# Two loads of the joined stage issued by ScalarE instead of SyncE

## The reference, cut to what matters

```python
def step(carry, inp):                      # one chunk: 16 tokens, 4 batches, 8 heads
    W1c, b1c = carry
    xq, xk, xv, et = inp
    Z1 = xk @ W1c + b1c
    grad = _ln_l2_bwd(Z1, xv - xk, g, bb)
    Attn1 = jnp.tril(xq @ xk.swapaxes(-1, -2))
    b1_bar = b1c - jnp.tril(et) @ grad
    Z1_bar = xq @ W1c - et * Attn1 @ grad + b1_bar
    last_eta = et[..., -1, :, None]
    W1n = W1c - (last_eta * xk).swapaxes(-1, -2) @ grad
    b1n = b1c - (last_eta * grad).sum(-2, keepdims=True)
    return ((W1n, b1n), xq + _ln(Z1_bar, g, bb, EPS_IN))
```

## Time and profile before

| | |
|---|---|
| median of 3 runs | 6032.22 us (6026.91 to 6053.81) |
| profiled execution | 6036.71 us |
| its span, first to last instruction | 6034.6 us |
| mean granted TensorE clock | 0.937 |
| busy: PE, PEld | 5435.4, 3858.9 us (90%, 64%) |
| busy: DVE | 3921.2 us (65%) |
| busy: ACT, POOL | 2358.1, 2375.7 us (39% each) |
| DMA queue 1 (SP's) | 613160 packets, 541.06 MB |
| DMA queue 10 (ACT's) | 157904 packets, 144.22 MB |

### The profile page before, as it was taken

How to read it: one execution, slowest core, us unless ns; L and a number is a source line. 1 busy time by engine, 2 the same in 40 slices (tenths; PEclk the granted TensorE clock), 3 DMA queues, 4 the chain that set the end, 5 groups by cost and what they waited for, 6 DMA issues and landing times. The chain is left out here.

```text
span 6034.6 us, 139327 instructions
## 1 busy us (share of the span) xinstructions
PE 5435.4 (90%) x42562; PEld 3858.9 (64%) x42562; DVE 3921.2 (65%) x14040; ACT 2358.1 (39%) x6645; POOL 2375.7 (39%) x3910
## 2 busy tenths in 40 slices
PE   5999999999688888898888888897899999599999
PEld 2444444444377777777777777777666666377777
DVE  5666666656677777777777777776566666444444
ACT  0111111111255555555555555554333333233333
POOL 1444444444355555555555555553112222122221
PEclk8999999999788988989889999998999999799999
DMA  4444444343345544545455455453212211122221
GB/s 176 159 142 143 138 155 144 120 130 124 105 118 124 126 121 124 125 123 125 122 125 127 120 127 127 126 127 93 113 77 90 89 62 61 66 91 90 90 90 72
DMA packets 771865, 694.46 MB, mean 115 GB/s; under 512 B 334160, under 2 KB 672472, under 8 KB 760184
## 3 DMA queue, kind: packets, MB, share of 16 engines
q1 hardware_dynamic: 613160, 541.06, 31.2%
q10 hardware_dynamic: 157904, 144.22, 7.1%
HBM read 402.96 MB, written 282.20 MB: 114 GB/s over the span
## 5 line engine op out<-in xcount | busy, mean ns | idle before, releaser
L1496 PE MATMUL proj_ps<-proj_w_sb,proj_h 128*128 128x512 f32 x3072 | 1351.1, 598 | 0.0
L1496 PEld LDWEIGHTS proj_ps<-proj_w_sb,proj_h 128*128 128x128 f32 x3072 | 580.4, 192 | 746.6 <-issue 727.4
L2287 PE MATMUL scan_ps_y<-scan_o_t,proj_wo_sb 128*128 128x128 f32 x4096 | 614.0, 296 | 2.1 <-ACT scan_o_t L1920 2.1
L1399 DVE SCALAR_TENSOR_TENSOR proj_lin<-proj_ps,proj_rstd,proj_wbias_sb 128x512 f32<-128x512 f32 x384 | 283.8, 747 | 500.9 <-PE proj_ps L1496 495.1
L1823 POOL TENSOR_TENSOR scan_b_step<-scan_core,scan_rate_last 128x128 f32<-128x128 f32 x512 | 321.9, 629 | 617.1 <-DVE scan_core L2076 616.8
L2287 PEld LDWEIGHTS scan_ps_y<-scan_o_t,proj_wo_sb 128*128 128x128 f32 x4096 | 532.2, 203 | 47.8 <-ACT scan_o_t L1920 2.6
L1884 ACT ACTIVATE scan_square<-scan_ps_z 128x64 f32<-128x64 f32 x1024 | 217.9, 219 | 719.4 <-PE scan_ps_z L2205 700.1
L1877 ACT COPY scan_state_w<-scan_ps_w 128x512 f32<-128x512 f32 x480 | 280.8, 585 | 328.1 <-PE scan_ps_w L2217 323.4
L2217 PE MATMUL scan_ps_w<-scan_step,scan_record 64*128 64x128 f32 x4088 | 383.1, 310 | 24.5 <-DVE scan_step L2081 23.6
L1308 POOL TENSOR_TENSOR proj_by_cos<-proj_lin,proj_rope 128x512 f32<-128x512 f32 x256 | 333.2, 1315 | 167.9 <-DVE proj_lin L1399 126.0
L2055 DVE TENSOR_TENSOR scan_zg<-scan_ps_z,scan_gain 128x128 f32<-128x128 f32 x512 | 145.9, 285 | 386.2 <-ACT scan_square L1884 326.0
(11 more groups left out here) (317 smaller groups left out, 12143.3 us busy)
## 6 DMA issues: line engine op xcount, KB each, us to landing
scan_record<-records SPq DMA_DIRECT2D x258, 392.0 KB
records<-proj_rec ACTq DMA_DIRECT2D x256, 392.0 KB, 3.6
spectra<-fourier_spec SPq DMA_DIRECT2D x16, 2112.0 KB, 6.5
fourier_spec<-spectra SPq DMA_DIRECT2D x16, 2112.0 KB, 8.2
scan_k_in<-records SPq DMA_DIRECT2D x258, 128.0 KB, 5.3
proj_h<-x SPq DMA_DIRECT2D x32, 1024.0 KB, 6.6
queries<-proj_q ACTq DMA_DIRECT2D x128, 256.0 KB, 3.7
gradients<-scan_stored SPq DMA_DIRECT2D x512, 64.0 KB
```

The costliest lines, as they stand in the source:

```text
L1399: v.scalar_tensor_tensor(lin[q][:, n], ps[q][n][:], rstd[k][:, j:j + 1], T.wbias[:, n], ALU.mult, ALU.add).then_inc(lin_sb.sem, 1)
L1496: last = pe.matmul(ps[j % 2][n][:], h[k][:, ct, j * P:(j + 1) * P], T.w[:, n, ct], start=ct == 0, stop=ct == CT - 1)
L2287: pe.matmul(ps_y[:, n], T.wo[:, ct, n * P:(n + 1) * P], o_t[:, ct], start=ct == 0, stop=False)
```

## The change

The second load of the keys, and the load of the queries, leave SP's body and stand in ACT's. The keys: in every even step but the very first (c = 0 included), between `leave` and `outputs_turned`, for the slot that has just ended, with the same wait for `turn_k`. The queries: at c = 4, right behind the keys, instead of at c = 3. SP's last wait for `k_loaded` goes to ACT. The load that the last odd step issued for a tile beyond the end is gone with it (one of 129).

```diff
--- SP's body
-                elif scan:
-                    if c == 3:
-                        if isinstance(v, int) and not p:
-                            sp.wait_ge(turn_k.sem, turn_k.at(B, 0))
-                        if not isinstance(v, int):
-                            sp.wait_ge(qb_sb.sem, qb_sb.at(v * 8 + p * 4 - 4, 0))
-                        sp.dma_start(q_sb[p][:]..., q_in[:, bass.ds((v * 2 + p) * P, P)]...).then_inc(q_loaded[p].sem, 16)
-                    b, n = (c // 2 + 1) % B, p + 1 + (c // 2 + 1) // B
-                    sp.wait_ge(turn_k.sem, turn_k.at(v * 8 + at.slot + 1 + B, 0))
-                    load_keys(k_in[:], k_loaded, b, v * 2 + n)
--- ACT
+            def load_keys(at):
+                b, n = (at.slot + 1) % B, 1 + (at.slot + 1) // B
+                act.wait_ge(turn_k.sem, turn_k.at(at.v * 8 + at.slot + 1 + B, 0))
+                for n2 in range(2):
+                    act.dma_start(k_in[:].rearrange("p (a n) e -> p a n e", n=2)[:, :, n2],
+                                  rec[:, bass.ds((at.v * 2 + n) * P, P), n2, b, n2 * HD:(n2 + 1) * HD].rearrange("a t e -> t a e")
+                                  ).then_inc(k_loaded.sem, 16)
+            def load_queries(at):
+                if isinstance(at.v, int) and not at.p:
+                    act.wait_ge(turn_k.sem, turn_k.at(B, 0))
+                if not isinstance(at.v, int):
+                    act.wait_ge(qb_sb.sem, qb_sb.at(at.v * 8 + at.p * 4 - 4, 0))
+                act.dma_start(q_sb[at.p][:]..., q_in[:, bass.ds((at.v * 2 + at.p) * P, P)]...).then_inc(q_loaded[at.p].sem, 16)
--- ACT's body, even steps
                     if gone:
                         leave(gone)
+                    if scan and not (isinstance(at.s, int) and at.s == 0):
+                        load_keys(Place(at.v, at.p, at.c - 1) if at.c else Place(at.v - 1 + at.p, 1 - at.p, 7))
+                    if scan and at.c == 4:
+                        load_queries(at)
                     if proj:
                         outputs_turned(proj)
```

More of the change, by code:

```diff
@@ L1779, in body @@
                                 "o (a t n) e -> n (o t) a e", n=2, t=CS)[n]).then_inc(grad_in[q].sem, 16)
-                elif scan:
-                    if c == 3:
-                        if isinstance(v, int) and not p:
-                            sp.wait_ge(turn_k.sem, turn_k.at(B, 0))
-                        if not isinstance(v, int):
-                            sp.wait_ge(qb_sb.sem, qb_sb.at(v * 8 + p * 4 - 4, 0))
-                        sp.dma_start(q_sb[p][:].rearrange("p b h e -> p b (h e)"), q_in[:, bass.ds((v * 2 + p) * P, P)].rearrange("b n c -> n b c")
-                                     ).then_inc(q_loaded[p].sem, 16)
-                    b, n = (c // 2 + 1) % B, p + 1 + (c // 2 + 1) // B
-                    sp.wait_ge(turn_k.sem, turn_k.at(v * 8 + at.slot + 1 + B, 0))
-                    load_keys(k_in[:], k_loaded, b, v * 2 + n)
             loop(sp, body)
@@ L1800, in _ @@
                     sp.wait_ge(grad_gone[g][q].sem, grad_gone[g][q].at(SC * 4, 0))
-            sp.wait_ge(k_loaded.sem, k_loaded.at(TILES + 1, 0))
             for q in range(2):
@@ L1908, in _ @@
             state_out(0, Place(0, 0, 0))
+            def load_keys(at):
[10 more added lines that the diff above has]
+                    act.wait_ge(qb_sb.sem, qb_sb.at(at.v * 8 + at.p * 4 - 4, 0))
+                act.dma_start(q_sb[at.p][:].rearrange("p b h e -> p b (h e)"), q_in[:, bass.ds((at.v * 2 + at.p) * P, P)].rearrange("b n c -> n b c")
+                              ).then_inc(q_loaded[at.p].sem, 16)
             def normed(tile):
@@ L2009, in _ @@
             loop(act, body)
+            act.wait_ge(k_loaded.sem, k_loaded.at(TILES, 0))
         @block.vector
```

## The result

The changed kernel took 5939.93 us (median of 4, 5930.72 to 5945.14) against 6035.81 us (median of 4) for the one before: a ratio of 0.9836, 95% interval 0.9809 to 0.9862, so 96 us faster. The forecast was 5922 us. Nearly all of it lies in the joined stage.

The account below looks back on a forecast made before the run. PE was taken as nearly full but partly at its lower clock, with b_in late behind SP's full queue. From 6036.71 us, -190 + 32 + 48 = -110 gave 5926.7, less 4.5 for the runs' median: 5922 us, range 5790 to 6170.

Parts of the forecast that it names:

- ACT's room: Time ACT may spend on the loads in an even step before PE's next projection is late: about 2.6 us.
- The whole, 337 us: Joined stage: time over 256 clean steps of 8.585 us, all that a change of issue order can win.
- 267 to be won: Upper bound of SP's relief: 226 us for late b_in plus 41 us for late keys and records.
- the signs named for "right": PE's b_in wait under 25 us, granted clock about 0.96, ACT's key pair about 2 us, no new PE wait.
- The relief of SP, -190 us: Key and query loads leave SP's queue, so b_in, keys and records come earlier: 170 plus 20 us won.
- three quarters of 226: Share of b_in's cost in the joined stage (89.7 us of wait times 2.5) taken as won: 170 us.
- The price of 2.5 us for each us of a wait: On PE, one 2.43 us wait for b_in cost 6.12 us with the lower clock; applied to all b_in waits.
- the no-change rival: Transfers, not SP's turn, make b_in late, wherever issued: 6032 give or take 30 us; chance 0.16.
- ACT's side, +80 us: Cost on ACT in even steps: 32 us for the queries and 48 us for the pair beside SP's bursts.
- the hold beside SP's bursts, +48 us: ACT's issues held by SP's x_in and y bursts, 1 and 0.5 us past ACT's room, 32 times each.
- The slower rival: ACT is held in even steps, its key pair costing 4.3 us: +135 us, about 6167 us; chance 0.28.

Follow-up runs that it names:

- e1: The changed kernel with the queries' load back in SP's queue, only the keys on ACT: 5941.34 us, ratio 0.9869 to the kernel before.
- e2: The kernel before with only the queries' load moved to ACT at c = 4: 5989.31 us, ratio 0.9951.
- e6: The changed kernel with four more ACT copies of 128x512 behind the loads: 5926.88 us, ratio 0.9855 to the kernel before.
- e11: The changed kernel with x_in, y's store and the queries in parts over odd steps, keys behind ACT's state copy: 5813.83 us, ratio 0.9648 to the kernel before.
- e10: The kernel before with the 1 MB load of x_in cut into quarters, everything still on SP: 5979.13 us, ratio 0.9922.
- e4: The kernel before without the second loads of the keys and their wait, outputs not the reference's: 5829.18 us, ratio 0.9687.
- e5: The changed kernel with two more ACT copies of 128x512 behind the loads: 5922.94 us, ratio 0.9861 to the kernel before.
- e7: The changed kernel with ACT's key and query loads moved behind the state copy at the even step's end: 5878.82 us, ratio 0.9777 to the kernel before.
- e9: The changed kernel with keys issued by ACT behind the state copy and the queries back on SP: 5915.55 us, ratio 0.9819 to the kernel before.
- e12: As e11, but SP issues everything, with the keys where the kernel before has them: 5941.13 us, ratio 0.9871 to the kernel before.

## Why the prediction was right, and where it wasn't

**Right**: that b_in is late, and with it PE's clock; that the keys' and queries' issues in SP's queue are a cause (e1, e2); that the pair hides in ACT's room (2.6 us assumed, 2.6 to 3.3 by e6). The whole, 337 us, of which 267 to be won, isn't contradicted: e11 wins 208 us. But that the forecast came within 18 us of the measured time is luck: one term was twice too large, and another, of the other sign, was nothing. Two of the signs named for "right" didn't come: b_in's wait is 58.4 us, not under 25, and the stretch's clock 0.93, not 0.96.

**The relief of SP, -190 us, was twice too large.** Measured are 96. The step that failed is "three quarters of 226": b_in's wait fell by a third (89.7 to 58.4), not by three quarters. Besides, the wait for DVE's step, which the sum didn't have, grew by 34 us. The price of 2.5 us for each us of a wait came from a single step, and e10, with 17.6 us more of b_in's wait and 43 us less time, shows that it can't be laid on the sum. I had the no-change rival, that descriptors drain as slowly wherever they were issued, as an alternative to the forecast. It is a part of it: e4 puts the price of the keys at 189 us, of which the move wins 79 (e1) and leaves 110, by my reading to the transfers.

**ACT's side, +80 us, doesn't show**, and this hid the first error. 1.2 us more of work on ACT cost nothing (e5), though ACT does stand behind its own loads: its copy of the turned outputs waits for them 92 times, 69.6 us in all, where it didn't before. And e1, without the queries on ACT, isn't faster than the change (0.9869 against 0.9836). The pair took 2 x 0.51 = 1.0 us, not 1.87, I take it because ACT's queue is nearly empty when it issues. The queries took 0.49 by the median instead of 1.10. And the hold beside SP's bursts, +48 us, rested on two issues of the projection stage that end together; in the stage itself ACT's longest issue of a key load ended 2.0 us before SP's. The slower rival hung on the same reading: its pair would have cost 4.3 us. The Trainium skill's rule in "Perfetto Trace Analysis", section "DMA Instruction — HWDGE (DVE, Sync)" (the descriptor generator is locked for one sequencer at a time), doesn't hold in the strict form that I gave it, that ACT stands through SP's long issues. Whether ACT's issues grow beside SP's at all is open: they take 0.54 us on the mean beside one and 0.46 alone in the kernel after, but 0.45 and 0.53 in e7.

**The shared engines.** Transfers in one queue delay those in the other: e9 shows keys on ACT made later by the queries on SP. The Trainium skill, page "DMA: Bandwidth & Descriptors", section "Issuing engines are not separate DMA queues", says that a second issuing engine saves the sequencer's time alone, usually small; this is nearer to the runs than my weight of it. But the issue time isn't small here: 444 us of SP's time in the stage for keys and queries, and moving them gave 1.6% of the kernel.

**What I could have seen in the rows**: that SP's long issues (2.81 us for stores which take 1.32 otherwise) are in part the transfers before them, still unfinished. I summed them as SP's work. e10 bears this out: with the same stores, and x_in alone cut in four, the longest fell from 8.9 to 2.2 us.

## What to carry to other kernels

Before moving a DMA to another queue, ask what its issue time on the old one consists of. The part above the shortest issue of the same load (0.37 of 0.98 us here) is, by my reading, largely other transfers draining, and some of it comes back in the issues that stay behind: a third here. The change of queue (1.6%), the order of the loads (0.6%) and the size of each (0.8%) are three levers, and e11 with all of them gave 3.5%. A load that is needed late should be issued after the one that is needed soon. A 1 MB transfer between small ones is best cut into parts and spread over the steps, if the queue has room: the quarters of the queries took 0.35 us each to issue on ACT (e11) and 2.56 on SP (e12).

## What was not expected of the hardware

ACT did 2.2 us more work in 121 steps (e6) and the kernel took the same time: one wait of PE grew by 67 us, two others shrank by 21 and 29. A 256 KB load took 0.35 us to issue on one queue and 2.56 us on the other, at the same steps. And in one step a wait of 2.4 us, beside a granted clock of 0.50, cost 6.1 us, so that removing a wait early in a step can be worth over twice its length.
